# A macaron block on one core: W1 and W2 turned first, small weights moved between engines, new orders in the lead and the first image

## What is computed

```python
x = x + 0.5 * _ffn(_layernorm(x), W1, b1, W2, b2, scale)
x = x + _attn(_layernorm(x), Wq, Wk, Wv, Wproj, q_rms_w, k_rms_w, omega, u)
x = x + 0.5 * _ffn(_layernorm(x), W1, b1, W2, b2, scale)

# _attn
q, k = rmsnorm(q) * q_rms_w, rmsnorm(k) * k_rms_w
u_n  = u / max(norm(u), 1e-6)
gate = softplus(einsum(k, u_n) / 8)
bias = -max(i - j, 0) * softplus(omega) * slopes * gate[j]      # -inf where j > i
y    = softmax(q @ k.T / 8 + bias) @ v
return y @ Wproj
```

## Time and profile before

| | |
|---|---|
| median of three runs | 761.49 us |
| the profiled execution | 761.77 us |
| its span, first to last instruction | 759.9 us |
| TensorE busy | 731.5 us, 96% |
| VectorE busy | 656.4 us, 86% |
| ScalarE busy | 640.2 us, 84% |
| GpSimd busy | 645.7 us, 85% |

### The profile page before, as it was taken

The page is one execution under the profiler, slowest core; times in us unless marked ns, Lnnn a source line. Parts: engine busy times, 40 slices in busy tenths (PEclk is TensorE's granted clock), DMA queues, the critical chain, the costliest instruction groups (busy, mean ns, idle before and its releaser), DMA issues.

```text
span 759.9 us, 25094 instructions
## 1 busy us (share of the span) xinstructions
PE 731.5 (96%) x9299; PEld 526.1 (69%) x9299; DVE 656.4 (86%) x2105; ACT 640.2 (84%) x1420; POOL 645.7 (85%) x753
## 2 busy tenths in 40 slices
PE   4889999999999999999999999999999999999987
PEld 2356767677767777687667777577776876777765
DVE  8799888988988888988989889897889879899976
ACT  5768888888998889887998889988898879986673
POOL 6537879989998989989899899989899899997690
PEclk9989999999999999999999999999999999999999
DMA  5332424253343514454143532435133430534431
GB/s 153 61 87 70 87 44 103 56 100 73 62 96 85 101 30 91 89 101 92 26 105 71 100 73 54 103 80 108 29 86 89 108 88 21 109 72 105 95 44 30
DMA packets 99618, 60.33 MB, mean 79 GB/s; under 512 B 74622, under 2 KB 86400, under 8 KB 99496
## 3 DMA queue, kind: packets, MB, share of 16 engines
q1 hardware_dynamic: 99336, 58.19, 36.1%
q10 hardware_dynamic: 160, 0.52, 0.3%
HBM read 4.74 MB, written 2.10 MB: 9 GB/s over the span
## 4 chain that ended last, share of the span: by engine, by line
PE 67%; DVE 14%; ACT 13%; issue 4%; POOL 2%; DMA 1%; DVEq 0%; ACTq 0%; POOLq 0%
PE ps L1089 12%; PE ps L1090 11%; PE ps L1091 11%; PE ps L1220 7%; PE ps L1246 7%; PE ps L1247 7%; PE ps L1202 5%; DVE masked L1588 4%; ACT qk L1025 3%; PE ps L1248 3%; DVE ss L1553 3%; ACT pt L1050 2%; PE ps L1106 1%; ACT hid L967 1%; ACT qkn L978 1%
## 5 line engine op out<-in xcount | busy, mean ns | idle before, releaser
L845 POOL TENSOR_TENSOR pt_l<-pt 128x512 f16<-128x512 f32 x366 | 321.4, 906 | 34.4 <-ACT pt L1050 32.5
L1588 DVE CUSTOM_DVE_ANT_0 masked<-ps,causal_row 128x512 f16<-128x512 f32 x448 | 192.1, 486 | 26.0 <-PE ps L1220 25.1
L1050 ACT ACTIVATE pt<-ps 128x512 f32<-128x512 f32 (+1 forms) x384 | 174.8, 535 | 17.2 <-PE ps L1248 15.1
L871 POOL TENSOR_TENSOR qkn<-qkn,rs 128x512 f32<-128x512 f32 x128 | 129.9, 1043 | 28.9 <-ACT rs L989 28.3
L1246 PE MATMUL ps<-qk 128*128 128x512 f16 (+3 forms) x512 | 146.6, 299 | 0.0
L1247 PE MATMUL ps<-qk 128*128 128x512 f16 (+3 forms) x512 | 146.5, 299 | 0.0
L1089 PE MATMUL ps<-v_buf,pt 128*128 128x65 f16 x1280 | 129.8, 194 | 2.6 <-POOL pt_l L845 1.2
L1090 PE MATMUL ps<-v_buf,pt 128*128 128x65 f16 x1280 | 129.8, 193 | 0.0
L1091 PE MATMUL ps<-v_buf,pt_l 128*128 128x65 f16 x1280 | 129.6, 193 | 0.0
L1089 PEld LDWEIGHTS ps<-v_buf,pt 128*128 128x128 bf16 x1280 | 118.0, 98 | 8.4 <-issue 4.9
L1090 PEld LDWEIGHTS ps<-v_buf,pt 128*128 128x128 bf16 x1280 | 117.5, 98 | 1.8
(11 more groups left out here) (212 smaller groups left out, 1966.6 us busy)
## 6 DMA issues: line engine op xcount, KB each, us to landing
qk<-qk SPq DMA_DIRECT2D x128, 128.0 KB, 2.4
qk<-qk SPq DMA_DIRECT2D x62, 256.0 KB, 3.7
x_in<-in_L_attn_x SPq DMA_DIRECT2D x8, 256.0 KB, 3.2
out<-x_out SPq DMA_DIRECT2D x7, 256.0 KB, 2.4
qk<-qk SPq DMA_DIRECT2D x1, 1024.0 KB, 7.5
qk<-gtt SPq DMA_DIRECT2D x64, 8.0 KB
qk<-nmt SPq DMA_DIRECT2D x64, 2.0 KB
y_hl<-ytt SPq DMA_TRANSPOSE x62, 3.2
```

The lines of the kernel that those rows point to most:

```text
L845: g.tensor_tensor(pt_l[:, h % 2, c], pt[:, h % 2, c], pt_h[:, h % 2, c], ALU.subtract).then_inc(s_pt_l, 1)
L871: g.tensor_tensor(qk, qk, r.unsqueeze(4).broadcast_to([P, 2, 2, 2, D]), ALU.mult).then_inc(s_qkn, 1)
L1050: a.activation(pt[:, h % 2, c], ps[:, j, 0:width], ACT.Exp).then_inc(s_exp, 1)
L1588: ins = d.tensor_tensor_reduce(masked[:, part.unit(s, i)[0], col:col + (ib + 1) * P], part.bank(s, i)[:, col:col + (ib + 1) * P], causal_r ...
```

## The change

1. TensorE turns W1 and W2 first, then the normalized tokens. Their two loads get a semaphore of their own, and VectorE's scaling becomes the stage `w12`, ahead of `setup`. `zt` waits for `sc_up` alone, and `m` for the scaled weights.
2. The constant rows are made by ScalarE, ahead of all its other work.
3. `gate_factors` becomes a GpSimd stage (`gf`, five small operations); VectorE's `m` no longer holds it.
4. Of the gate weights `gu2` keeps the product and the sum. `wu_h` is made by ScalarE and `wu_l` by GpSimd (stages `wu`). `uu` and `gu2` move ahead, and `wq` 0 and 1 on VectorE move back.
5. `b2rows` has one copy of 128 columns instead of four.
6. In image 0 the heads 8 to 15 are masked by VectorE, no longer by TensorE.
7. New orders in `lead` and `first` on all engines; `body` and `final` are as they were.

```diff
         "lead": [      # tensor, after
+            ("setup", NEXT), ("zt", "a", NEXT), ("m", "a", NEXT), ("warm", 0, 6, NEXT), ("h", "a", NEXT),
+            ("out", "a", NEXT), ("warm", 1, 4, NEXT), ("uu", NEXT), ("warm", 1, 5, NEXT), ("zt", "att", NEXT),
+            ("warm", 1, 3, NEXT), ("qk", 0, 0, NEXT), ("qk", 0, 1, NEXT), ("qk", 0, 2, NEXT), ("qk", 0, 3, NEXT),
+            ("v", 0, 0, NEXT), ("qk", 1, 0, NEXT), ("v", 0, 1, NEXT), ("qk", 1, 1, NEXT), ("warm", 1, 6, NEXT),
+            ("qk", 1, 2, NEXT), ("qk", 1, 3, NEXT), ("t", 0, NEXT), ("gl", 0, NEXT), ("warm", 1, 2, NEXT),
+            ("t", 1, NEXT), ("qk", 2, 0, NEXT), ("qk", 2, 1, NEXT), ("warm", 1, 5, NEXT), ("gr", 0, NEXT),
+            ("t", 2, NEXT), ("t", 3, NEXT), ("qk", 2, 2, NEXT), ("qk", 2, 3, NEXT), ("a", 0, NEXT), ("a", 1, NEXT),
+            ("qk", 3, 0, NEXT), ("a", 2, NEXT), ("a", 3, NEXT), ("qk", 3, 1, NEXT), ("v", 0, 2, NEXT),
+            ("nm", 0, NEXT), ("v", 0, 3, NEXT), ("qk", 3, 2, NEXT), ("qk", 3, 3, NEXT), ("a", 4, NEXT),
+            ("s", 0, NEXT), ("a", 5, NEXT), ("s", 1, NEXT), ("a", 6, NEXT), ("gl", 1, NEXT), ("pv", 0, NEXT),
+            ("a", 7, NEXT), ("t", 4, NEXT), ("nm", 1, NEXT), ("v", 1, 0, NEXT), ("t", 5, NEXT), ("t", 6, NEXT),
...
         "lead": [      # vector, after
+            ("ln1", "a", NEXT), ("ln2", "a", NEXT), ("zl", NEXT), ("us", NEXT), ("w12", NEXT), ("setup", NEXT),
+            ("zt", "a", NEXT), ("m", "a", NEXT), ("uu", NEXT), ("h", "a", NEXT), ("add", "a", NEXT),
+            ("ln1", "att", NEXT), ("ln2", "att", NEXT), ("wq", 0, NEXT), ("zt", "att", NEXT), ("gu2", 0, NEXT),
+            ("qk", 0, 0, NEXT), ("gu2", 1, NEXT), ("qk", 0, 1, NEXT), ("qk", 0, 2, NEXT), ("qk", 0, 3, NEXT),
+            ("qk", 1, 0, NEXT), ("v", 0, 0, NEXT), ("qk", 1, 1, NEXT), ("wq", 1, NEXT), ("v", 0, 1, NEXT),
...
         "first": [     # tensor, after (part)
+            ("s", 5, THIS), ("m", "a", NEXT), ("pv", 4, THIS), ("a", 10, THIS), ("s", 6, THIS), ("h", "a", NEXT),
+            ("a", 11, THIS), ("wp", 0, THIS), ("out", "a", NEXT), ("nm", 2, THIS), ("v", 1, 2, THIS), ("pv", 5, THIS),
+            ("s", 7, THIS), ("a", 12, THIS), ("v", 1, 3, THIS), ("pv", 6, THIS), ("zt", "att", NEXT), ("s", 8, THIS),
...
         "first": [     # sync, after
+            ("ln1", "a", NEXT), ("rows", 2, THIS), ("gd", 2, THIS), ("swap", 2, THIS), ("back", 2, THIS),
+            ("rows", 3, THIS), ("gd", 3, THIS), ("yt", 0, THIS), ("yt", 1, THIS), ("nm", 2, THIS), ("yt", 2, THIS),
+            ("yt", 3, THIS), ("nm", 3, THIS), ("swap", 3, THIS), ("back", 3, THIS), ("rows", 0, NEXT),
...
-        def masked_by_dve(b, ib):
-            return b > 0
+        def masked_by_dve(b, h):
+            return b > 0 or h >= HH
...
+            def gate_factors(part, s, b):      # GpSimd
+                pool.wait_ge(s_oml, 2)
+                g.tensor_scalar(om_e[:, :], om[:, :], 0.0, None, ALU.max).then_inc(s_factors, 1)
+                g.tensor_tensor(omr[:, :], om_e[:, :], om_n[:, :], ALU.add).then_inc(s_factors, 1)
+                g.tensor_tensor(omr[:, :], omr[:, :], slopes[:, :], ALU.mult).then_inc(s_factors, 1)
...
+            def unit_weights_lo(part, s, b, hf):      # GpSimd
+                pool.wait_ge(s_wu_h, hf + 1)
+                g.tensor_tensor(wu_l[:, heads], wu[:, heads], wu_h[:, heads], ALU.subtract).then_inc(s_prepared, 1)
...
+            act.wait_ge(s_icol, 1)                    # ScalarE, first of all
+            a.activation(rows16[0:5, :, :], icol[0:5, :].unsqueeze(1).broadcast_to([5, 2, T]), ACT.Copy, scale=0.0,
+                         bias=1.0).then_inc(s_rows_one, 1)
+            act.wait_ge(s_rows_one, 1)
+            a.activation(rows16[0:2, :, :], icol[0:2, :].unsqueeze(1).broadcast_to([2, 2, T]), ACT.Copy).then_inc(s_rows16, 1)
...
             def setup(part, s, b):                    # TensorE
-                pe.wait_ge(s_wffn, 16 * 7)
+                pe.wait_ge(s_w12, 32)
...
-            link(d.memset(rows16[0:5, :, :], 1.0))
-            dve.wait_ge(s_icol, 1)
-            d.tensor_copy(rows16[0:2, :, :], icol[0:2, :].unsqueeze(1).broadcast_to([2, 2, T])).then_inc(s_rows16, 1)
+            def first_weights(part, s, b):
                 dve.wait_ge(s_w12_ps, 2 * FB)
                 d.tensor_scalar(w1s[:, :], ps[:, 0, :], W_UP, None, ALU.mult)
                 d.tensor_scalar(w2s[:, :], ps[:, 1, :], W_UP, None, ALU.mult).then_inc(s_setup, 1)
...
-                link(d.tensor_copy(wu_h[:, heads], wu[:, heads]))
-                d.tensor_tensor(wu_l[:, heads], wu[:, heads], wu_h[:, heads], ALU.subtract).then_inc(s_prepared, 1)
-                dve.wait_ge(s_prepared, hf + 1)
+                d.tensor_reduce(wu[:, heads], of_heads(uk[:, half_of]), AX.X, ALU.add).then_inc(s_wu, 1)
```

More of the change, by code:

```diff
@@ L29 @@
         "lead": [
[L30 to L34, removed]
@@ new lines @@
+            ("rows", 0, NEXT), ("qk", 2, 1, NEXT), ("t", 2, NEXT), ("t", 3, NEXT), ("qk", 2, 2, NEXT),
+            ("qk", 2, 3, NEXT), ("qkn", 2, 0, NEXT), ("qk", 3, 0, NEXT), ("rows", 1, NEXT), ("wu", 1, NEXT),
+            ("qk", 3, 1, NEXT), ("nm", 0, NEXT), ("v", 0, 2, NEXT), ("v", 0, 3, NEXT), ("qkn", 2, 1, NEXT),
+            ("qk", 3, 2, NEXT), ("qk", 3, 3, NEXT), ("s", 0, NEXT), ("s", 1, NEXT), ("qkn", 3, 0, NEXT),
+            ("qkn", 3, 1, NEXT), ("gate", 1, NEXT), ("t", 4, NEXT), ("nm", 1, NEXT), ("v", 1, 0, NEXT),
@@ new lines @@
+            ("qkn", 0, 1, NEXT), ("qk", 1, 1, NEXT), ("qk", 1, 2, NEXT), ("qk", 1, 3, NEXT), ("nm", 3, THIS),
+            ("qkn", 1, 0, NEXT), ("qkn", 1, 1, NEXT), ("v", 0, 1, NEXT), ("v", 0, 2, NEXT), ("gate", 0, NEXT),
+            ("s", 10, THIS), ("t", 0, NEXT), ("t", 1, NEXT), ("s", 11, THIS), ("v", 0, 3, NEXT), ("t", 2, NEXT),
+            ("t", 3, NEXT), ("qk", 2, 0, NEXT), ("s", 12, THIS), ("yt", 4, THIS), ("qk", 2, 1, NEXT), ("s", 13, THIS),
+            ("qkn", 2, 0, NEXT), ("qk", 2, 2, NEXT), ("yt", 5, THIS), ("qk", 2, 3, NEXT), ("qk", 3, 0, NEXT),
@@ L254 @@
         "lead": [
-            ("weights", NEXT), ("clear", NEXT), ("rows", 0, NEXT), ("gd", 0, NEXT), ("gd", 1, NEXT),
-            ("rows", 1, NEXT), ("swap", 0, NEXT), ("swap", 1, NEXT), ("back", 0, NEXT), ("nm", 0, NEXT),
+            ("weights", NEXT), ("clear", NEXT), ("rows", 0, NEXT), ("gd", 0, NEXT), ("rows", 1, NEXT),
+            ("swap", 0, NEXT), ("gd", 1, NEXT), ("back", 0, NEXT), ("nm", 0, NEXT), ("swap", 1, NEXT),
             ("back", 1, NEXT), ("nm", 1, NEXT),
@@ L497, in macaron @@
         y_last = y_end[1]
+        s_w12 = sem("s_w12")
         s_wffn = sem("s_wffn")
@@ L1016, in gate_softplus, with unit_weights_hi @@
                 a.activation(lgl[:, :, :], lge[:, :, :], ACT.Ln, bias=1.0).then_inc(s_lgl, 1)
+            def unit_weights_hi(part, s, b, hf):
+                heads = slice(hf * HH, (hf + 1) * HH)
+                act.wait_ge(s_wu, hf + 1)
+                a.activation(wu_h[:, heads], wu[:, heads], ACT.Copy).then_inc(s_wu_h, 1)
             def hi_parts(part, s, b, p):
                 if b == 0 and p == 0:
-                    act.wait_ge(s_prepared, 1)
+                    act.wait_ge(s_wu, 1)
                     act.wait_ge(s_wv_lo, 1)
@@ L1139, in ffn_out @@
                     width = T // 2 if shared(n, b) else T
-                    pe.matmul(dst[:, first:first + width], ones[:, :], b2rows[:, :, :].rearrange("p t c -> p (t c)")[:, first:first + width],
+                    pe.matmul(dst[:, first:first + width], ones[:, :], b2rows[:, :].unsqueeze(1).broadcast_to([P, width // C, C]),
                               start=True, stop=False)
```

208 lines of the change are left out of this document (91 added, 117 removed).

## The result

The changed kernel took 755.68 us in the median of four runs (755.65 to 756.5); the kernel before, beside it, 761.66 (760.38 to 761.85). The ratio is 0.9922, with a 95% interval of 0.9908 to 0.9937: 6.0 us less. The profiled execution took 755.66 us (span 753.9). Against that of before (761.77) that is 6.11 less, and it lies here: 5.03 ahead of scores 2 of image 0, 0.81 from there to scores 0 of image 1, 0.20 in all that follows, 0.07 around the span.

What follows compares the result with a forecast made beforehand. It took the lead to be bound by a chain over engines and the rest by TensorE's work. Lead 3.4 plus masks 1.8 made 5.2 off 761.77, forecast 756.5 us (chance 0.50), range 753.9 to 759.8.

Steps and rivals of the forecast that it cites:

- the transfer of the maxima: In the lead, from the transpose of the maxima to scores 0: 4.1 to 4.7 us, scores 0 at 57.5 to 57.9.
- the masks: First image: eight heads lose their four causal matmuls on TensorE, 1.8 us less, 0 as the other end.
- (a): Rival: the masks' gain in the first image is handed back to waits, only the lead's 3.4 is left: 758.4 us; chance 0.18.
- (b): Rival: the clock falls again in the lead, up to 1.7, and the held q/k weight costs 1.0 more: 759.2 us; chance 0.11.
- (c): Rival: everything by TensorE's bound, lead 4.4, masks 1.8, order 0.5: 755.1 us; chance 0.11.
- Start: Start of the lead: 1.2 us off for the constant rows, 2.2 in all; weff at 9.98 against 12.20; b2 rows cost nothing.
- FFN output: First FFN in the lead: COPY off VectorE, w_l not held by memsets, first product at 15.65 against 18.44: 2.8 us.
- First projection: Attention's first q/k projection on TensorE moves from 26.84 to 24.15: 2.7 us.
- Turned heads: First turned heads start at 35.0 against 38.95, 3.9 us, with 1.2 paid for the q/k weight among qkn.
- Gates and maxima: In the lead: gate rows at 42.0 against 45.61, first score maxima at 46.2 against 49.79, four heads end at 53.1.
- The lead's sum: Scores 2 of the first image at 68.3: the lead is 3.4 us shorter, bounds 2.4 to 4.4.
- (d): Rival: SyncE's queue delays the y transposes in the first image, 5.2 + 1.5 are lost, 763.3 us; chance 0.05.

Runs made afterwards that it cites:

- e9: The changed kernel with the constant rows filled and cast by VectorE at its start, as before: 757.8 us, ratio 0.9959.
- e11: The kernel before with W1 and W2 turned first, constant rows on ScalarE and VectorE's first stages in the new order: ratio 1.0005.
- e4: The kernel before with VectorE's COPY of the gate factors made a maximum of the value with itself, two SBUF inputs: ratio 1.0001.
- e8: The changed kernel with the gate factors back in VectorE's adapted-weights stage, as before: 756.56 us, ratio 0.995.
- e1: The kernel before with one edit, heads 8 to 15 of image 0 masked by VectorE: ratio 1.0004.
- e6: The changed kernel with VectorE's second low part of the query weights moved ahead of GpSimd's six qkn operations: 754.67 us, ratio 0.9925.
- e5: The changed kernel with wu_h (ScalarE) and wu_l (GpSimd) put before and between the first qkn groups: 754.84 us, ratio 0.9928.
- e2: The changed kernel with the masks of image 0 all by TensorE again: 757.65 us, ratio 0.9953.
- e10: The changed kernel without seven filler matmuls behind the first gate logits and the projection (2,1): 755.18 us, ratio 0.993.
- the repeat: The changed kernel run once more, unedited, as the measure for three runs beside it: 756.98 us, ratio 0.9947.
- e3: The changed kernel with the old `first` order lists on every engine, new lead lists and VectorE's masks kept: 756.95 us, ratio 0.9939.

## Why the prediction was right, point by point

The time, 755.7, lies 0.8 us under the forecast, but two of its terms, the transfer of the maxima and the masks, were wrong, in opposite directions. That they nearly cancel is luck. (The chances of the forecast and of (a), (b) and (c) add up to 0.90; the prediction has 0.89.)

**Start.** weff at 9.67 (I had 9.98), right: both the fills and the turned weights. Of my 1.2 for the fills e9 shows 0.9: x landed later (the statistics start at 3.66, not 3.5), and e9's start at 4.56, not at 4.73. That b2 "costs nothing" holds for the 128 columns; that they were a precondition I had not seen. With 512 they are the next late thing, by 1.6 us (e11: 12.56 against 10.93).

**FFN output.** First product 15.30 (I had 15.65), w_l 0.69 as predicted. The cause needs a correction: without the COPY w_l isn't held (e4), but in the new order it isn't late with the COPY either (e8), because VectorE waits for w_h. The length of the hold in the earlier trace rows was one execution's: its COPY took 2.80, that of e1 1.01, and the output started 1.0 earlier. The Trainium skill's rule ("SBUF — State Buffer", "Who interferes with whom") that a VectorE operation with two SBUF inputs is not held by a GpSimd instruction that only writes SBUF agrees with e4's 0.23 us beside the memsets.

**First projection.** 23.91 (I had 24.15), unit u at 19.22, right.

**Turned heads.** 34.40 (I had 35.0). The hold of qkn by the query weights is real: 1.0 us on GpSimd, seen in 7.06 against 6.04. I had paid 1.2; taking it away gives 0.9 at t0 (e6). The Trainium skill's rule, in the same section, that the shared port pair is an exclusive lock, agrees with the fourth qkn, which started 0.06 us behind VectorE's 1.21 us operation and took 2.06 instead of 1.04, and with 3.04 against 2.13 at 21.86. The 1.0 more than in my sum did not come: VectorE's own operation came first and took 1.21, unheld.

**Gates and maxima.** Gate rows 41.51 (42.0), a0 45.28 (46.2), the transpose of the maxima 52.34 (53.1). TensorE's waits for wu_l and gt were as described, and of the first 0.5 us was still to be had at s2 (e5). From the gate rows to the maxima it was 3.77, where I had taken 4.18 from the earlier trace rows; 0.4 of the early a0 lies there.

**Scores.** Here is the mis-sized term of the lead. I let the transfer of the maxima take 4.1 to 4.7 us, from 62.65 - 57.91 in the earlier trace rows. After, the two starts are 3.31 apart, with TensorE at work but for one wait of 0.34 for v_buf and none at scores 0, so the transfer takes 3.31 at most. What stood between the two starts in before was TensorE's own queue (three projections, one of them v's, and two maxima heads) and not the transfer; so the distance of 4.74 was no measure of the transfer, and the lower end of 4.1 that I took from it no bound. Scores 0 came at 55.65 instead of 57.7 and scores 2 at 66.69 instead of 68.3; between the two lie 11.0 us, where I had 10.6.

**The lead's sum**, 5.03 against 3.4, is also partly a matter of which execution was profiled. e1 and e4, whose lead is that of before, reach s2 at 69.4: 1.0 of the 2.3 by the shorter hold (all starts from the output to t0), the rest from t0 to the gate rows, where they had one fall of 3.41 us and before 6.83. Taking 1.1 off for that fall, the lead of before would reach s2 near 68.3, and the change is worth some 1.6 us in the lead by order and work: an estimate from two executions, to which the spread of x's landing (0.4) adds.

**First image.** Of 1.8 for the masks, 0.2 (e1) to 0.5 (e2) arrived. The count and the pace were right: TensorE needs 0.79 us for a head's four products with the masks (56.96 to 57.75 in after) and 0.54 without (92.78 to 93.32), which makes 2.0 for the eight. Two steps failed. One is "There the time is TensorE's work", taken from a busy share of 79.64 in 80.70. The other is that VectorE's masked maximum "costs nothing that shows", taken from VectorE's share: a head takes VectorE 0.34 us longer, and in e1 TensorE then waits 1.4 us for the maxima, where it waited 0.4. That is rival (a), in the main, for which I had written that such stretches have no spare wait. In the changed kernel the 0.9 for qkn is there without the edit, too (e2); of its waits those for hid and z_hl (0.4 and 0.3) are not in e2. The new order gave nothing, as predicted.

**Rivals.** (b) did not occur in the first profiled execution, but it does in others: of the nine further ones with the new lead, e8's has the fall in the lead, for 1.1 us, and 8 of the 52 executions have a mean clock of 0.996 or below, with falls that can lie anywhere. The seven fillers taken out in e10 weren't what held it up: without them two of five executions have no fall at all. The other 24 are not tested. (d), SyncE's queue: nothing in the waits of after's first image names the y transposes, but the repeat and e9 each have one wait of TensorE for them (0.5 and 0.4 us), so they are close to late. The forecast's 5.2 thus came from 3.4 that should have been less by order and more by clock, and 1.8 that should have been 0.5 to 0.8.

What stays open: why executions with the new lead are without a fall so much more often, also in the last image, whose lists are the same; and what decides whether a COPY is held to the end of one memset or of all.

## What to carry to other kernels

A distance between two starts is a bound of a transfer only where TensorE waits for it: look for the wait's row before using the distance as a term. A busy share of 98.7% doesn't say that removed work returns as time; do the removal alone, since in e1 nine tenths of it came back as waits, for the engine that took the work over. When starts of two executions are compared, count from the first one that a load sets: here it moved by 0.4 us, which hid 0.4 of e6's gain of 1.0. And before a stall or a gain is costed from one profiled execution, see whether it is there in a second one: the hold of the COPY and the length of the clock's falls were not.

## What the runs showed of the hardware that was not expected

- A VectorE COPY beside four memsets of GpSimd (3.63 to 3.67 us in all) took 1.01, 1.05, 2.80 or 3.55 us, in four executions. It ended with the second memset or with the last.
- A VectorE operation with two SBUF inputs (1.21 us) that runs among GpSimd's qkn multiplications adds 1.0 us to them and loses nothing itself (1.21 there, 1.22 in e6, where it runs ahead of them).
- The granted clock fell in the last image in some executions of kernels whose last image is the same code (0, 3.41 or 6.83 us), at up to 1.3 and 2.4 us of time.
- Image 2, the same code in all kernels, took 89.5 to 89.6 us in some executions (after, e3, e6 to e9), 88.7 to 88.9 in others (e2, e4, e5, e10, e11, the repeat) and 89.1 in before and e1; TensorE's wait is put down to issue (0.6 us after, 0.8 in e6). No wait for another engine was found there.
- A masked maximum on VectorE comes with a second operation that reads the accumulator out, 86 ns each, four a head.
- x landed at another time in each execution: the statistics that wait for it started at 3.42 to 3.81 us.
